# Attention output by DMAs in token order, second norm one round earlier, in a decoder layer on one core

## The reference

```python
attn = jax.nn.softmax(attn + mask, axis=-1)             # causal
out = jnp.einsum('bnqk,bnkh->bnqh', attn, v)
out = out.reshape(B, -1, S)                             # (B, 256, 256), no transpose before it
return jnp.einsum('bds,nhd->bsd', out, W_out)
```

## Time and profile before

| | |
|---|---|
| runs | 971.19, 968.09, 965.02 us; median 968.09 |
| profiled execution | 962.93 us, span 961.2 us |
| mean granted TensorE clock | 0.967 of full speed |
| PE busy | 887.1 us (92% of the span) |
| DVE busy | 586.2 us (61%) |
| POOL busy | 496.3 us (52%) |
| ACT busy | 487.4 us (51%) |
| DMA, all queues | 92.96 MB, 133197 packets, 75712 of them under 512 B |

### The profile page before, as it was taken

The page is one execution under the profiler, slowest core; times in us unless marked ns, Lnnn a source line. Parts: engine busy times, 40 slices in busy tenths (PEclk is TensorE's granted clock), DMA queues, the critical chain, the costliest instruction groups (busy, mean ns, idle before and its releaser), DMA issues.

```text
span 961.2 us, 31757 instructions
## 1 busy us (share of the span) xinstructions
PE 887.1 (92%) x11966; PEld 653.0 (68%) x11966; DVE 586.2 (61%) x1292; ACT 487.4 (51%) x839; POOL 496.3 (52%) x705
## 2 busy tenths in 40 slices
PE   5999999999997689899998988999999999999995
PEld 3667667667665356565564776778888888878783
DVE  4856766766764456777777657455555555555552
ACT  3667677677666367566455542333333333333331
POOL 2556666566565333366666667534444434444432
PEclk9999999999999799999888899999999999999998
DMA  9222443443445654455453233433332333233322
GB/s 283 70 57 67 93 129 90 96 127 90 92 119 121 172 183 132 146 177 179 144 162 118 90 86 89 87 62 51 48 51 47 53 49 52 46 52 52 47 34 23
DMA packets 133197, 92.96 MB, mean 97 GB/s; under 512 B 75712, under 2 KB 114112, under 8 KB 132928
## 3 DMA queue, kind: packets, MB, share of 16 engines
q1 hardware_dynamic: 119760, 73.10, 28.2%
q0 software_dynamic: 13296, 17.83, 11.1%
HBM read 54.65 MB, written 37.32 MB: 96 GB/s over the span
## 4 chain that ended last, share of the span: by engine, by line
PE 80%; DVE 7%; ACT 5%; issue 3%; DMA 2%; SPq 2%; another core or an unknown queue 1%; POOL 0%; DVEq 0%; ACTq 0%; POOLq 0%
PE pair L933 19%; PE pair L949 12%; PE pair L951 6%; PE pair L634 5%; PE pair L671 5%; PE pair L657 4%; PE pair L811 3%; PE pair L607 3%; PE pair L684 2%; PE pair L825 2%; PE pair L829 2%; PE pair L861 2%; PE pair L900 2%; PE pair L786 1%; PE pair L837 1%
## 5 line engine op out<-in xcount | busy, mean ns | idle before, releaser
L933 PE MATMUL pair<-XTs,WU 128*128 128x128 bf16 x3408 | 283.9, 219 | 5.9 <-DVE XTs L1269 2.9
L933 PEld LDWEIGHTS pair<-XTs,WU 128*128 x3408 | 238.1, 98 | 71.7 <-issue 8.7
L1603 POOL DMA_INDIRECT out_d<-XB x71 | 116.1, 1635 | 207.4 <-DVE XB L1291 174.0
L949 PE MATMUL pair<-WD,Hh 128*128 x568 | 214.8, 379 | 1.3 <-issue 1.3
L1469 ACT ACTIVATE Hf<-pair 128x512 f32<-128x512 f32 x142 | 84.8, 597 | 219.5 <-PE pair L933 207.9
L1282 DVE CAST Hh<-Hf 128x512 bf16<-128x512 f32 x142 | 64.5, 454 | 172.1 <-ACT Hf L1469 166.9
L951 PE MATMUL pair<-WD,Hl 128*128 x568 | 154.7, 272 | 0.0
L1284 DVE TENSOR_TENSOR Hl<-Hf,Hh 128x512 bf16<-128x512 f32 x142 | 99.5, 701 | 4.9
L1514 POOL TENSOR_SCALAR_AFFINE_SELECT PT<-PT 128x512 f32<-128x512 f32 (+1 forms) x96 | 73.9, 787 | 44.2 <-ACT PT L1320 28.7
L1576 POOL DMA_INDIRECT xs_scr<-XB,WGf x64 | 66.9, 1045 | 31.7 <-issue 18.2
L1488 POOL TENSOR_TENSOR LS<-LS,mhalf 128x2 f32<-128x2 f32 x48 | 34.1, 711 | 94.6 <-DVE LS L976 93.9
(11 more groups left out here) (243 smaller groups left out, 1728.9 us busy)
## 6 DMA issues: line engine op xcount, KB each, us to landing
...
STG<-wup_in SPq DMA_DIRECT2D x32, 256.0 KB
...
STG<-wdn_in SPq DMA_DIRECT2D x32, 256.0 KB
o_scr<-On SPq DMA_DIRECT2D x32, 128.0 KB, 4.2
Mm<-o_scr SPq DMA_DIRECT2D x16, 256.0 KB, 3.0
CnT<-ctxt_in SPq DMA_DIRECT2D x16, 256.0 KB, 4.0
CX<-ctx_in SPq DMA_DIRECT2D x16, 256.0 KB, 4.4
```

The lines of the kernel that those rows point to most:

```text
L933: t = e.matmul(upb(j, k)[:, 128 * (fm % 4):128 * (fm % 4) + 128], WU[:, bass.ds(reg[j] * 4096 + off, 128)], XTs[:, r, hx, dk, :], start=n ...
L949: e.matmul(yb[r][:, 0:512], Hh[:, r, hsl], WD[:, bass.ds(reg[i] * 4096 + 512 * fk, 512)], start=fk == 0, stop=False, skip_group_check=True)
L1603: e.indirect_dma_start(out=out, out_offset=bass.IndirectOffsetOnAxis(ap=XS[:, i % NX, 256:257].bitcast(I32), axis=0), in_=Yf[:, i % NY, :] ...
```

## The change

ACT's copy of PV to `OTs` permutes the free dimension, so that each partition holds its elements by token group s = q mod 16, then head of its group, then q // 16. The heads of Q and K are permuted on the host (`places`), so that group j holds heads 4j to 4j + 3 and each run of 64 elements is contiguous in the output. A4, `On`, `Mm`, the transposes L702, L693 and L877 and their pair of banks are gone. In their place: OT, one DMA of the sums to `dnc`, 128 partitions of 32, and four of the output to `o_scr` in 256-byte pieces, in token order; RC, DVE's reciprocal and product with `wsq`, now 128x32; WB, four DMAs of the factors to DRAM (`rsc`); XA, one DMA reading the output back with tokens on partitions; BC, two DMAs reading the factors back, each row of 256 to the 16 partitions that share it, into `XR`; X1, DVE's product XA * XR and the addition to x. The second norm is done for block i - 3 instead of i - 4. All five orders of `ROUND` are new; those of `ORDER` stay. The setup of `wsq` takes one pass instead of two.

```diff
 ROUND = {
-    "tensor": "AX:1 MG:1 S1:0:0 T0:1:0 PV:2 S1:0:1 QK:-1 T0:1:1 S0:0 VX:0 T2:1 GT:15 weights:1:2 A4:2",
-    "vector": "Gp:16 weights:-2:0 A6s:4 weights:-1:1 S1:0:1 S0:0 VX:0 A4:2 weights:1:2 MG:0 AX:0 S1:-1:0 Gs:15 A0s:-3",
-    "scalar": "PV:2 A0n:-2 QK:-1 T0:1:1 Gt:13 A6c:4 weights:-2:0 A6n:4 VX:0 T2:1 weights:-1:1 AX:0 GT:15 MG:0 T0:0:0",
-    "gpsimd": "weights:0:2 split:0 T0:1:0 T0:1:1 split:0 GT:15 T2:1 A6c:4 A0s:-3 A6s:3",
-    "sync": "GT:15 load:0 A4:3 AX:1 Go:16 queries:16 decays:16",
+    "tensor": "MG:1 S1:0:0 T0:1:0 PV:2 S1:0:1 QK:-1 T0:1:1 S0:0 VX:0 T2:1 GT:15 weights:1:2 AX:0",
+    "vector": "A0s:-2 X1:3 S1:0:1 weights:-2:0 Gp:16 A6s:3 weights:-1:1 S0:0 weights:1:2 RC:2 Gs:15 MG:0 AX:0 S1:-1:0",
+    "scalar": "PV:2 A0n:-2 weights:-2:0 Gt:13 A6c:3 QK:-1 T0:1:1 VX:0 weights:-1:1 A6n:3 T2:1 AX:0 GT:15 MG:0 T0:0:0",
+    "gpsimd": "split:0 T0:1:0 A6s:3 T0:1:1 GT:15 weights:0:2 A6c:3 split:0 T2:1 A0s:-3",
+    "sync": "load:0:1 GT:15 BC:3 queries:16 load:0:0 AX:1 Go:16 OT:2 decays:16 XA:2 WB:2",
 }
 
-LIMITS = {"S1": (0, B - 1), "T0": (0, B - 1), "PV": (0, B - 2), "A0s": (0, B - 1), "A0n": (0, B - 1), "QK": (0, B - 1), "A6s": (0, B - 4),
-          "A6n": (0, B - 4), "S0": (0, B - 1), "VX": (0, B), "T2": (0, B - 1), "A6c": (0, B - 4), "A4": (0, B - 2), "AX": (-2, B), "MG": (0, B)}
+LIMITS = {"S1": (0, B - 1), "T0": (0, B - 1), "PV": (0, B - 2), "A0s": (0, B - 1), "A0n": (0, B - 1), "QK": (0, B - 1), "A6s": (0, B - 3),
+          "A6n": (0, B - 3), "S0": (0, B - 1), "VX": (0, B - 1), "T2": (0, B - 1), "A6c": (0, B - 3), "X1": (0, B - 3), "OT": (0, B - 2), "XA": (0, B - 2),
+          "RC": (0, B - 2), "WB": (0, B - 2), "BC": (0, B - 2), "AX": (-2, B), "MG": (0, B)}
...
             if kind == "load":
                 if ok(b):
-                    yield kind, 2 * b, 0
-                    yield kind, 2 * b + 1, 0
+                    yield kind, 2 * b + u, 0
...
     yield "PV", B - 1, 0
-    yield "MG", B + 1, 0
-    yield "A4", B - 1, 0
+    yield "OT", B - 1, 0
     yield "contexts", 0, 0
+    yield "queries", 1, 0
+    yield "WB", B - 1, 0
+    yield "XA", B - 1, 0
     yield "decays", 1, 0
-    yield "queries", 1, 0
     yield "contexts", 1, 0
+    yield "BC", B - 1, 0
 
 
 def attention_rest():
 
     z = B - 1
-    return {(0, 0): (("A6s", z - 2), ("Mm", z), ("X1", z - 1), ("A6n", z - 2), ("A6c", z - 2)),
-            (0, 1): (("A6s", z - 1), ("XQ", z - 2), ("A6n", z - 1), ("A6c", z - 1)), (0, 2): (("X1", z), ("A6s", z)),
-            (1, 0): (("GA", z - 2), ("A6n", z)), (1, 1): (("XQ", z - 1), ("A6c", z)), (2, 0): (("XQ", z),), (2, 1): (("GA", z - 1),),
-            (3, 0): (("GA", z), ("Gt", 1)), (3, 1): (("GT", 1),), (3, 2): (("Gs", 1),), (4, 2): (("GE", 1),), (5, 0): (("Gp", 1),),
-            (5, 1): (("Go", 1),)}
+    return {(0, 0): (("RC", z), ("X1", z - 1), ("A6s", z - 1), ("A6n", z - 1), ("A6c", z - 1),), (0, 1): (("GA", z - 2), ("XQ", z - 1),),
+            (0, 2): (("X1", z), ("A6s", z),), (1, 0): (("A6n", z), ("A6c", z), ("GA", z - 1),), (1, 1): (("XQ", z),),
+            (2, 0): (("GA", z), ("Gt", 1),), (2, 1): (("GT", 1),), (2, 2): (("Gs", 1),), (3, 2): (("GE", 1),), (4, 0): (("Gp", 1),),
+            (4, 1): (("Go", 1),)}
...
-                                    c = 17 * (8 * a + 2 * j + par)
+                                    c = 17 * (4 * j + 2 * a + par)
...
-                elif kind == "A4":
-                    pair_free(w, "A4", b)
-                    ps = pair_of("A4", b)
-                    w.wait_ge(ot_.sem, ot_.at(b))
-                    for tt in range(2):
-                        for g in range(4):
-                            o = ps[:, tt, 256 * (g // 2):256 * (g // 2) + 256].rearrange("p (j r c) -> p j r c", j=4, r=2)[:, :, g % 2, :]
-                            t = e.transpose(o, OTs[:, g, 128 * tt:128 * tt + 128], idf)
-                    t.then_inc(oT.sem, 1)
...
+        def vector_denominators(e, w, b):
+            w.wait_ge(l_dc, 16 * (b + 1))
+            w.wait_ge(l_wb, 64 * b)
+            e.reciprocal(dnc[:, :], dnc[:, :]).then_inc(dvc.sem, dvc.up())
+            w.wait_ge(dvc.sem, dvc.n)
+            e.tensor_tensor(rc[:, :], dnc[:, :], wsq[:, :], ALU.mult).then_inc(rc_.sem, 1)
+
+        def vector_residual(e, w, b):
+            r = b % 2
+            w.wait_ge(l_xa[r], 16 * (b // 2 + 1))
+            w.wait_ge(l_bc, 32 * (b + 1))
+            e.tensor_tensor(XA[:, r, :, :], XA[:, r, :, :], XR[:, :, :], ALU.mult).then_inc(dvc.sem, dvc.up())
+            w.wait_ge(dvc.sem, dvc.n)
+            e.tensor_tensor(xb(b), XA[:, r, :, :], xb(b), ALU.add).then_inc(x1_.sem, 1)
...
-                elif kind == "VX" and ok(b - 3):
-                    m = b - 3
-                    w.wait_ge(mT.sem, mT.at(m))
-                    e.tensor_tensor(xb(m), pair_of("VX", b)[:, 1, :].rearrange("p (t c) -> p t c", t=2), xb(m), ALU.add).then_inc(x1_.sem, 1)
-                elif kind == "A4":
-                    bv = pair_of("A4", b)[:, :, :].rearrange("p t (n c) -> p t n c", c=32)
-                    w.wait_ge(oT.sem, oT.at(b))
-                    w.wait_ge(l_o, 32 * b)
-                    e.reciprocal(bv[:, :, :, 16], bv[:, :, :, 16]).then_inc(dvc.sem, dvc.up())
-                    w.wait_ge(dvc.sem, dvc.n)
-                    e.tensor_tensor(rc[:, :, :], bv[:, :, :, 16], wsq[:, :, :], ALU.mult).then_inc(dvc.sem, dvc.up())
-                    w.wait_ge(dvc.sem, dvc.n)
-                    e.tensor_tensor(On[:, :, :, :].rearrange("p t n c -> p (t n) c"), bv[:, :, :, 0:16].rearrange("p t n c -> p (t n) c"),
-                                    rc[:, :, :].rearrange("p t (n a) -> p (t n) a", a=1).broadcast_to([128, 2 * NH, 16]),
-                                    ALU.mult).then_inc(on_.sem, 1)
+                elif kind == "RC":
+                    vector_denominators(e, w, b)
+                elif kind == "X1":
+                    vector_residual(e, w, b)
...
                 elif kind == "PV":
                     w.wait_ge(pv.sem, pv.at(b))
-                    w.wait_ge(wsq_, 2)
-                    w.wait_ge(oT.sem, oT.at(b - 1))
-                    e.activation(OTs[:, :, :], pair_of("PV", b)[:, :, :].rearrange("p a (r c) -> p (a r) c", r=2), ACT.Copy).then_inc(ot_.sem, 1)
+                    w.wait_ge(wsq_, 1)
+                    w.wait_ge(l_ot, 64 * b)
+                    w.wait_ge(l_dc, 16 * b)
+                    e.activation(OTs[:, :, :].rearrange("p g c -> p (g c)").rearrange("p (s g d) -> p s g d", s=16, g=4),
+                                 pair_of("PV", b)[:, :, :].rearrange("p a (r d s) -> p s (a r) d", r=2, s=16), ACT.Copy).then_inc(ot_.sem, 1)
...
             for kind, b, P in sp_attn:
                 if kind == "load":
                     load_chunk(e, w, b)
-                elif kind == "A4":
-                    w.wait_ge(on_.sem, on_.at(b))
+                elif kind == "OT":
+                    w.wait_ge(ot_.sem, ot_.at(b))
+                    w.wait_ge(rc_.sem, rc_.at(b - 1))
+                    e.dma_start(dnc[:, :], OTs[16:128:32, :, :].rearrange("p g c -> p (g c)").rearrange("p (s c) -> p s c", c=32)).then_inc(l_dc, 16)
+                    ov = osc[b, :].rearrange("(s h d) -> h s d", s=16, h=16)
+                    for j in range(4):
+                        e.dma_start(ov[:, :, 64 * j:64 * j + 64], OTs[32 * j:32 * j + 16, :, :].rearrange("p g c -> p (g c)").rearrange(
+                            "p (s c) -> p s c", s=16)).then_inc(l_ot, 16)
+                elif kind == "XA":
+                    w.wait_ge(l_ot, 64 * (b + 1))
+                    w.wait_ge(x1_.sem, x1_.at(b - 2))
+                    e.dma_start(XA[:, b % 2, :, :], osc[b, :].rearrange("(t p d) -> p t d", t=2, p=128)).then_inc(l_xa[b % 2], 16)
+                elif kind == "WB":
+                    w.wait_ge(rc_.sem, rc_.at(b))
+                    for j in range(4):
+                        e.dma_start(rsc[b, :].rearrange("(s j k c) -> j s k c", s=16, j=4, k=2)[j], rc[32 * j:32 * j + 32, :]).then_inc(l_wb, 16)
+                elif kind == "BC":
+                    w.wait_ge(l_wb, 64 * (b + 1))
+                    w.wait_ge(x1_.sem, x1_.at(b - 1))
                     for tt in range(2):
-                        e.dma_start(osc[b, :].rearrange("(n t p h) -> t p n h", n=NH, t=2, h=16)[tt], On[:, tt, :, :]).then_inc(l_o, 16)
-                    if b < B - 1:
-                        merged(e, w, b)
+                        e.dma_start(XR[:, tt, :], rsc[b, 2048 * tt:2048 * tt + 2048].rearrange("(s a d) -> s a d", s=8, a=1).broadcast_to(
+                            [8, 16, 256])).then_inc(l_bc, 16)
                 elif kind == "AX":
-                    if ok(b - 4):
-                        queries_out(e, w, b - 4)
                     if ok(b - 3):
-                        contexts_t(e, w, b - 3)
+                        queries_out(e, w, b - 3)
+                    if ok(b - 2):
+                        contexts_t(e, w, b - 2)
...
```

(2 more changed lines are left out.)

111 lines of the change are left out of this document (43 added, 68 removed).

## The result

The changed kernel takes 979.89 us (median of 20 runs, 971.44 to 988.21), the one before, in the same comparison, 969.08 (20 runs, 963.12 to 975.82). The ratio is 1.0107, 95% interval 1.0084 to 1.0129: slower by 10.8 us, where 10.7 us of gain were forecast. One per cent is 9.7 us. The profiled execution of the changed kernel has a span of 973.1 us, against 961.2.

A forecast was written before the change was run, and what follows sets the result against it. TensorE was taken to bound the middle attention rounds and a chain of waits the hand-over to mLSTM. Rounds 8.0 plus hand-over 2.7 gave 10.7 us, so the median 968.09 becomes 957.4; range 949 to 970.

The forecast's parts named there:

- PE's part: Attention rounds: 12 transposes removed per block, 1.46 us of TensorE work; T0 would start at 16.65 instead of 18.1.
- what is late next: Attention rounds: ACT's chain, then DVE's, holds T0, so a round goes from 18.1 to 17.3 us, 0.8 paid out.
- Rival (a): Attention rounds: ACT's chain shortens too and PE gets all 1.46 us, 6 us more gain, 951; chance 0.13.
- DVE's part: Attention rounds: VectorE's work stays equal but moves; X1 may end as late as 6.5, against 5.03 where it costs nothing.
- ACT's strided copy: ScalarE's PV copy reads PSUM with a stride; bounds 0 and twice its 1.02 us, taken as 0.
- SP and the new DMA chain: Attention rounds: SP has room for twelve issues per block; CnT lands at 5.6, needed by 7.1, so no wait.
- rival (b): Attention rounds: a new wait for X1 or CnT, some 0.6 a round, eats nearly all their gain, 964; chance 0.30.
- Two SBUF inputs: X1's two-SBUF-input operations on VectorE are held by GpSimd: 0.7 us for the pair, X1 ending near 5.6, inside 6.5.
- The hand-over: Attention to mLSTM: the 4.62 us wait for Mm goes, S:0:2's product comes 1.5 us earlier, leftovers give 1.2; together 2.7.
- (d): Rival at the hand-over from attention to mLSTM: transposes go but it gives 5 us back, 962; chance 0.08.
- rival (c): Attention rounds: the serial DRAM chain makes X1 end after 6.5, so slower, 985 or, at half, 977; chance 0.09.
- The signs of being wrong: Wrong if PE waits for S1's reduction or K's copy, or if the stretch around mLSTM's block 0 grows.

The follow-up runs named there:

- e1: The changed kernel with A6c moved behind T0's second pair of exponentials in ScalarE's order: 969.36 us, ratio 0.9996 to the kernel before.
- e7: e1 with the removed transposes put back as idle work, 8 and 4 per block: 982.21 us, ratio 1.0153 to the kernel before.
- e8: The kernel before with A6c (and once-used Gt) moved ahead of Q's and K's copies on ScalarE: 988.56 us, ratio 1.0244 to the kernel before.
- e9: e1, e3 and e4 together, with X1 moved behind S1's second reduction on VectorE: 942.78 us, ratio 1.0037 to the kernel before.
- e4: The changed kernel with block 15's RC one slot later and its WB stores behind the decay and context loads: 977.67 us, ratio 1.0084 to the kernel before.
- e3: The changed kernel with Gs and Gp back in their old places on VectorE: 975.12 us, ratio 1.0064 to the kernel before.
- e10: e9 with attention's leftovers in later mLSTM slots, Go behind OT, block 0's context load ahead of block 15's OT: 947.29 us, ratio 1.0078 to the kernel before.
- e11: e9 with SyncE's OT of block 14 ahead of Go and block 0's context load ahead of block 15's OT: 944.12 us, ratio 1.0051 to the kernel before.
- e15: e1, e3 and e4 together, with block 15's WB, XA and BC ahead of block 1's decays in SyncE's final list: 966.90 us, ratio 1.0003.
- e16: e15 with WB ahead of the decays and XA in SyncE's round as well: 979.32 us, ratio 1.0130 to the kernel before.

## Why the prediction was wrong

- **PE's part and what is late next: right.** 1.46 us were removed, the ACT chain was the next bound once nothing else held the round, and a round is worth 17.3 (17.34 in e1, gap ahead of T0 0.97 instead of 1.3). e7 gives the same 0.77 back. Rival (a), all 1.46 us, did not come up in any run.
- **DVE's part and ACT's strided copy: right.** S1's late reduction cost PE 0.3 us in eight rounds of the changed kernel. The copy took 1.02 us, as before.
- **SP and the new DMA chain: this step failed.** It put CnT's landing at 5.6 in round time against a need at 7.1. In the round from 187.26 it landed at 7.9, 2.3 later. Link by link: RC ended at 13.8 of the round before, not 13.4, most of it RC's held product (below). From there to the landing of r_scr it took 3.7 us, as forecast: four issues cost 2.5 us instead of 1.6, and the landing took 1.8 instead of 2.3. From that landing to CnT's issue it took 3.0 us instead of 1.7, since a broadcast load cost 0.63 and the store of the queries 1.04, where 0.41 each was set. CnT then took 4.8 to landing, not 4.2. The range that I gave (landing up to 8.7) held the truth, and I took its low end "since these pieces are small"; the issue costs do not shrink with the pieces.
- **The same step had a second flaw.** I read slack for each link against a fixed due time. But A6c stands ahead of K's copy, and K leads to S0 and to `rc_`: what comes late once comes late again a round later (RC ends at 14.4 in the round from 187.26). e8 shows that A6c's place alone costs the kernel before 20 us. Neither my forecast nor rival (b), which had this wait at 0.6 a round, followed it round.
- **Two SBUF inputs: over-priced for X1, and missed where it struck.** X1's products took 0.69 us, once 1.01, in the changed kernel, against 0.7 us of delay assumed. But RC's product, which had one input in PSUM and now has two in SBUF, is held in the rounds. Durations (min, median, max, ns) before and after, and one case in order of time:

```profile
L1041 DVE TENSOR_TENSOR rc<-pair,wsq x16: 190/191/192, 60.2 to 314.2; 128x32 f32<-128x32 f32 x16
```
```profile
L986 DVE TENSOR_TENSOR rc<-dnc,wsq x16: 191/574/874, 58.2 to 325.5; 128x32 f32<-128x32 f32 x16
```
```profile
201.04 0.61 POOL L1477 CAST WU<-STG 128x512 bf16<-128x512 f32 x1
...
201.12 0.57 DVE L986 TENSOR_TENSOR rc<-dnc,wsq 128x32 f32<-128x32 f32 x1
```

 It ends just behind the GpSimd cast. So some 0.4 us a round stand at the head of the DMA chain; the prediction named this ("up to 1.1, with the whole DMA chain behind it") and put nothing for it in the sum.
 The Trainium skill's rule (SBUF — State Buffer, "Who interferes with whom") fits these and e9's longer additions: in each the GpSimd instruction that ran when VectorE's began had ended before VectorE's did.
- **The hand-over: this step failed too,** and by more: 2.7 us of gain forecast, 9.2 us lost. PE's 4.62 us wait for Mm was removed, and waits of 9.90 and 4.47 took its place. What failed is the walk along the queues: it put the product of S:0:2 1.5 us earlier than before, and counted from T0(14) it came 9.9 us later (342.90 - 278.04, against 332.18 - 277.21). The count of the issues was not far off: nine more a block were set at 3.7 us; a block's twelve now take 6.5 (0.59 + 4 x 0.48 + 0.38 + 4 x 0.59 + 2 x 0.63), where the old three took some 2.1, so 4.4. The walk missed where they stand: in the last two blocks they are in one row with 16 decay loads, 5 loads of queries and 2 of contexts, and SP's queue has 8 us more of the chain than before. DVE, in order, stood 11.76 us in RC of block 15 for `dnc`, with X1 of block 14 and the product of S:0:0 behind it. This wait was in no term; e4, which takes it away, is not told apart from the changed kernel. Gs and Gp were named, and e3 shows some 4 us for them (0.43% of 968). I gave "4 us either way" for the walk, which was not from any row. That SP's queue is what holds is read from the chain; e10, e11, e15 and e16, which change its order, moved the wait and gained nothing at the end.
- **Rivals.** (b) came true for the rounds, (d) at twice its price for the hand-over. Each was priced with the other's gain kept. Together, by my own terms, they give 964 + 5 = 969, still 11 us under what was measured. The measured time lies in what rival (c) gave (977 to 985), but not by its mechanism: (c) needs X1 to end after 6.5 in round time, and in the round from 187.26 X1 ended at 5.3.
- **The signs of being wrong** were well chosen: PE waited for K's copy, 6.9 us in eight rounds, and the stretch around block 0 of mLSTM grew.

The last 2.4 us, from the experts' start to the end, go with the clock, in one execution each: over the first 120 us of the experts the granted clock is 0.97, before 1.00, with PE busy 111 us in both, and 3% of 120 is 3.6 us (an estimate).

How much of the loss from T0(14) on is the clock and how much the waits, no run separates. The mean granted clock of the runs is 0.953 in the changed kernel and 0.962 in the one before. It is 0.954 in e1, which is 1.1% faster than the changed kernel, so that difference is not the clock's. It is 0.957 in e8, where only the place of A6c was changed in the kernel before, so a lower clock comes with added waits alone.
